# Attention kernel: the twelve pieces of weighted sums of a half unit issued in six pairs

## What is computed

```python
scores = einsum('bhid,bhjd->bhij', q, k) * scale + gate * pos_bias
attn   = softmax(scores, axis=-1)
out    = einsum('bhij,bhjd->bhid', attn, v)
```

## Time and profile before

| | |
|---|---|
| median of three runs | 3783.45 us |
| profiled execution | 3788.6 us, span 3786.7 us |
| granted TensorE clock, mean over the span | 0.940 |
| attention, window 345 to 2343 us | 1998 us |
| PE, DVE, ACT, POOL busy, share of the span | 89%, 57%, 56%, 34% |

### The profile page before, as it was taken

The page is one execution under the profiler, slowest core; times in us unless marked ns, Lnnn a source line. Parts: engine busy times, 40 slices in busy tenths (PEclk is TensorE's granted clock), DMA queues, the critical chain, the costliest instruction groups (busy, mean ns, idle before and its releaser), DMA issues. The chain is left out here.

```text
span 3786.7 us, 61590 instructions
## 1 busy us (share of the span) xinstructions
PE 3360.6 (89%) x20980; PEld 2171.0 (57%) x20980; DVE 2150.9 (57%) x5133; ACT 2131.6 (56%) x4135; POOL 1305.1 (34%) x1788
## 2 busy tenths in 40 slices
PE   7994998989999999999999898685599999999992
PEld 4552444444444444444444443574588888888882
DVE  5765887878787878787778786376011111111115
ACT  4553887878787878787878787111222232232231
POOL 3333433333333333333333332037323223222221
PEclk9997999999999999999999999896799999999996
DMA  6666233343434333333343432663465565665666
GB/s 196 218 223 145 52 67 75 66 81 67 78 67 76 68 80 69 79 66 75 75 78 64 75 66 49 176 205 137 161 204 191 190 205 188 193 204 186 196 196 202
DMA packets 281897, 481.68 MB, mean 127 GB/s; under 512 B 59906, under 2 KB 166020, under 8 KB 263170
## 3 DMA queue, kind: packets, MB, share of 16 engines
q1 hardware_dynamic: 243970, 425.27, 42.1%
q0 software_dynamic: 26880, 35.87, 4.5%
q10 hardware_dynamic: 10752, 16.78, 1.2%
HBM read 323.47 MB, written 153.89 MB: 126 GB/s over the span
## 5 line engine op out<-in xcount | busy, mean ns | idle before, releaser
L745 DVE CUSTOM_DVE_ANT_0 tot<-sc,gbias 128x1024 f32<-128x1024 f32 x1024 | 1238.8, 1210 | 34.1 <-PE sc L645 19.8
L612 POOL TENSOR_SCALAR gbias<-slab_a,gs 128x484 f32<-128x484 f32 x1024 | 679.7, 667 | 1099.2 <-DVE negm L745 826.1
L797 ACT ACTIVATE probs<-tot,negm 128x640 f32<-128x640 f32 (+2 forms) x1024 | 766.0, 748 | 83.9 <-DVE negm L745 81.7
L645 PE MATMUL sc<-ks,qs 120*128 120x512 bf16 x2048 | 638.5, 394 | 181.7 <-DMA gs<-gate_d 153.2
L1305 ACT ACTIVATE f_hid<-f_ph,f_w_up 128x256 f32<-128x256 f32 x576 | 272.7, 473 | 722.4 <-PE f_ph L1266 722.4
L806 ACT ACTIVATE far_t<-fb 128x512 f32<-128x512 f32 (+1 forms) x1024 | 580.2, 567 | 124.2 <-PE fb L682 116.7
L757 DVE COPY near_t<-pb 128x256 f32<-128x256 f32 (+1 forms) x1024 | 397.5, 388 | 373.2 <-PE pb L666 366.1
L816 ACT ACTIVATE near_t<-pa 128x256 f32<-128x256 f32 (+1 forms) x1024 | 447.8, 437 | 209.7 <-PE pa L657 197.0
L1266 PE MATMUL f_ph<-f_xt,f_w_up 128*128 128x256 f32 x2304 | 511.9, 380 | 5.7 <-DMA f_w_up<-in_w_up 5.0
L1278 PE MATMUL f_py<-f_w_down,f_hid 128*128 128x256 f32 x2304 | 509.0, 379 | 0.0
L657 PEld LDWEIGHTS pa<-ident,probs 128*128 128x128 f32 x2560 | 335.5, 144 | 253.5 <-issue 111.9
(11 more groups left out here) (164 smaller groups left out, 3092.9 us busy)
## 6 DMA issues: line engine op xcount, KB each, us to landing
f_w_down<-in_w_down SPq DMA_DIRECT2D x72, 1152.0 KB, 5.3
f_w_up<-in_w_up SPq DMA_DIRECT2D x72, 1028.0 KB, 7.7
xg_d<-fill SPq DMA_DIRECT2D x113, 260.0 KB, 5.2
ks<-k_d SPq DMA_DIRECT2D x192, 128.0 KB
qs<-q_d SPq DMA_DIRECT2D x192, 128.0 KB
f_xin<-xg_d SPq DMA_DIRECT2D x72, 260.0 KB, 5.2
v_d<-vt SPq DMA_DIRECT2D x16, 1024.0 KB, 6.2
vs<-v_d SPq DMA_DIRECT2D x32, 512.0 KB, 11.8
```

Of the source, the lines that this page charges most:

```text
L612: pool.tensor_scalar(gbias[x % NG][:, SIDE:SIDE + BAND], slab[:, hh, :], gs[u % 2][:, i, hh:hh + 1], 1.0, ALU.mult, ALU.mult).then_inc(gbi ...
L645: mm = pe.matmul(sc[:, x % 2, c * 512:(c + 1) * 512], qs[u % 2][0:120, hh, i * P:(i + 1) * P], ks[u % 2][0:120, hh, c * 512:(c + 1) * 512] ...
L745: dve.tensor_tensor_reduce(tot[x % 2][:], sc[:, x % 2, :], gbias[x % NG][:, w:w + N], -1.0, 3.0e38, ALU.add, ALU.min, negm[h % 2][:, c:c + ...
L797: act.activation(probs[x % 2][:, 0:hi - lo], tot[x % 2][:, lo:hi], ACT.Exp, bias=negm[h % 2][:, c:c + 1], scale=-1.0).then_inc(near_done, 1)
```

## The change

One line. The number of pieces, their order and their sizes stay, and so does every wait; six steps of the sixteen have two pieces now, and ten have none. Before, ten steps had one piece, one had two (m = 6) and five had none.

```diff
-AV_STEP = (0, 2, 3, 5, 6, 6, 7, 9, 11, 12, 13, 14)
+AV_STEP = (0, 0, 2, 2, 4, 4, 7, 7, 11, 11, 14, 14)
```

## The result

The changed kernel took 3816.24 us (median of 6 runs, 3801.97 to 3824.72) against 3785.52 us before (6 runs): a ratio of 1.0079, 95% interval 1.0059 to 1.0098, 30.7 us slower. The profiled execution took 3815.34 us with a span of 3813.4 us. From PE's first matmul of the attention to its last the trace has 2058.3 us (344.5 to 2402.8), where it had 2030.0 (343.9 to 2373.8): 28.3 us more, and the spans differ by 26.7. So the whole loss lies in the attention. (It ends some 31 us behind 2343 and 2372, the ends of the windows, in both kernels.)

A forecast was written before the change was run, and what follows sets the result against it. PE leads with DVE and ACT close behind, and a unit is PE's steps 30 to 21 plus the load; 0.8 us more over 30 units and 2 us for the first two, taken as 25, gives 3808.5 us, range 3788 to 3832.

The forecast's parts named there:

- Pause and path: Attention: a unit takes PE's steps 30 to 21, then some 19 us of load; steps 22 to 29 change only the pause.
- Saved ends: PE's steps 30 to 21: 7 x 0.14 us for second pieces, 0.43 for two blocks moved; 1.41 us less work a unit.
- Waits of light runs: Steps without a piece in a row: PE waits for DVE's row, 2.0 us more a unit, plus 0.2 at steps 31, 0.
- The net of the path: PE's steps 30 to 21: 2.0 + 0.2 - 1.41 = 0.8 us more a unit.
- A: Attention: saved ends count, added waits don't come; faster, 3738 us, or 3771 if slack holds for half; 10%.
- B: Attention: saved ends and added waits cancel at about 1.4 us; no change, 3776 to 3791 us; 12%.
- C: Attention: PE's clock also falls in steps without a piece; 85 us slower, 3868 us; 4%.

The follow-up runs named there:

- beside_early_sums: Against the kernel before: pieces of 25 blocks of a unit in place of 15 in steps 22 to 29, and INV_AT 32 for 33; 3687.71 us, ratio 0.9738.
- alternate: Against the kernel before, AV_STEP alone: eight steps with pieces, never two steps without a piece in a row; 3787.47 us, ratio 1.0020.
- near_pairs: Against the kernel before, AV_STEP alone: near pieces as in the changed kernel, far ones as before; 3770.09 us, ratio 0.9974.
- dve_light_new: Changed kernel's AV_STEP, DVE's bias and maximum over near blocks alone (timing only); 3863.13 us, ratio 0.9984 to the kernel before; 3833.58 us with old steps.
- far_pairs: Against the kernel before, AV_STEP alone: far pieces as in the changed kernel, near ones as before; 3809.23 us, ratio 1.0083.
- new_early_sums: Changed kernel with INV_AT 32 for 33, so reciprocals and their spread come one step earlier; 3795.58 us, ratio 1.0025 to the kernel before.
- old_early_sums: Kernel before with INV_AT 32 for 33, so reciprocals and their spread come one step earlier; 3772.89 us, ratio 0.9961.
- beside_load: Against the kernel before, AV_STEP alone: pieces of 25 blocks of a unit in place of 15 in steps 22 to 29; 3749.74 us, ratio 0.9918.

## Why the prediction was right, and which terms were off

**Pause and path: right, with a flaw.** That a unit is PE's steps 30 to 21 and then the load, and that steps 22 to 29 are free, held in the experiments: beside_early_sums moved ten blocks there and its path fell by 2.8 us. But the time beside the load was not fixed at its length; it depends on the margin of the spread. This is the term that the prediction lacked: 0.35 us a unit, some 10 us of the 31. In the profile before it showed only in two late units (9.4 us of waits for `rcb` in 5), and I had passed that row by. It also broke a sign that I had set: the pause, 3.6 us before, was to stay within 0.5 us. It was 2.8 us on average over 29 units, and three of them had none.

**Saved ends: the mechanism right, the size too small.** I had read 0.14 us for a second piece from the start of a piece to the far matmul behind it, and 4 + 4 blocks agree with that (1.86 us against 2.00 for two alone). But this distance leaves out what a run of pieces costs ahead of its first matmul. Two neighbouring steps of before, the first light and the second with 4 blocks:

```profile
1233.17 0.38 PE L666 MATMUL pb<-ident,probs 128*128 128x128 f32 x2
1233.39 0.38 PE L682 MATMUL fb<-qs,ks 123*128 123x512 bf16 x1
...
1234.37 0.38 PE L666 MATMUL pb<-ident,probs 128*128 128x128 f32 x2
1234.68 1.06 PE L706 MATMUL po<-near_t,vs 128*32 128x512 f32 x8
1235.68 0.39 PE L682 MATMUL fb<-qs,ks 123*128 123x512 bf16 x1
```

From the transposes to the far matmul it is 0.22 us in the first and 0.31 + 1.00 in the second: 4 blocks cost 1.09, not 1.00. The distances of whole steps say the same: step 17 takes 1.20 us without a piece (alternate), 2.30 with 4 blocks (before) and 3.16 with 4 + 4 (after), so the first piece costs 1.10 and the second 0.86. A second piece saves 0.24 us, and PE's own work on the path fell by 7 x 0.24 + 0.43 = 2.1 us a unit, not 1.41 (an estimate from these steps, at full clock). The 0.1 us for each end also accounts for the 0.4 us that alternate (4 ends) came out below its count, and for 0.3 of the some 0.7 us in near_pairs (3 ends). The rule of the Trainium skill that I had cited, in "TensorEngine Tiling (Array Packing)", Key Properties, names a drain at a change of tiling mode. The trace agrees, with 0.09 us ahead of a run of pieces and 0.15 behind it, and PE's busy time fell by 29 us. What it makes of the time depends on the engines behind.

**Waits of light runs: right in place, too small in size, partly wrong in name.** Steps 3, 4, 7, 19 and 20 took 1.43, 1.34, 1.61, 1.66 and 1.47 us. The same steps without a piece take 0.98, 0.93, 1.21, 1.15 and 1.15 in the kernels where they are shortest, so they waited 0.3 to 0.5 us each, 2.1 in all where I had counted 1.6; the first light steps, 2 and 18, kept 1.03 and 1.15. I had said that PE would be seen waiting for DVE's `negm`. It is seen waiting mostly for ACT's `far_t`, a tighter tie in the same chain, and dve_light_new shows that ACT's cycle is a bound of its own. Lightening one of two engines with like cycles brings little.

**The net of the path: 0.8 us forecast, 0.55 in this pair of traces, 0.75 in the clean pair** (45.19 less 44.44, old and new steps with the spread early, neither with a late one). With 2.1 us less own work, the waits on the path must have grown by about 2.9 us, where I had counted 2.2. Both terms were some 0.7 us a unit too small, 20 us each over 30 units, and they cancel: that the net was close is in part luck. In time this pair differs by 3795.58 - 3772.89 = 22.7 us; the forecast was 25 for the change as a whole. The total came out near 31. By the traces the late spreads added the rest; by the times alone, 30.7 and 22.7 can hardly be told apart, given the intervals.

**Rivals.** A (only the ends count) is refuted by far_pairs and new_early_sums. B (both cancel) needed waits 0.6 us a unit below my count or a saving of 0.20 us an end; the saving was even larger, but the waits grew with it, and the interval of the result excludes B's range. C (the clock in light runs) did not come: 1.00 in the stretch shown.

**Order or chance.** The write of the maxima that precedes the spread took over 2.5 us in 9 of the 32 units of the changed kernel and in none of before. new_early_sums, another execution with the same steps of pieces, has it in the same 9 units, and old_early_sums in none. So it comes with the order of the pieces and not by chance. With INV_AT 32 the spread is late in none of these units all the same.

**Not settled:** what makes that write take 3 us in place of 1.4 in just these units. No experiment held it apart.

## What to carry to other kernels

An engine that is busy 99% can still lose when its work is bunched: compare the cycle of the engines behind it with its own step without the bunched work, and count the steps in a row in which it would be the faster one. Where a transfer sets the period, find which of the steps lie beside it and put the movable work there first; here that, together with fewer steps that have pieces (8 of a half in place of 11) and the shorter pause, was worth 85 us (old_early_sums to beside_early_sums), nearly four times what the pairing cost. And read the cost of a kind of work from whole steps with and without it; a distance between two chosen instructions can leave a part out. Look also at the small transfer issued just ahead of the large one: when the margin between them shrinks, both land late.

## What the runs showed of the hardware

In the six kernels with INV_AT 33, a spread of 2 KB rows to 128 partitions was late in 59 of 62 units when issued less than 3 us ahead of the load of 16 transfers, in 5 of 36 with 3 to 3.55 us, and in none of 76 with more. With a pause of 1.7 to 1.8 us on average before a unit (beside_load, beside_early_sums) the granted clock is 0.98 over the attention, with one of 3.6 us (before, old_early_sums) 0.96. A run of pieces on 32-column groups between full-width matmuls costs 0.24 to 0.25 us beyond its blocks (0.213 us each), however many pieces it has: some 0.1 us ahead of it and 0.15 behind.
